# A recommender tower: steps of 256 samples, with the products of earlier steps between the lookups

## The chip, the cores and the metric

One core of one Trainium2 chip runs the whole program. The metric is the device time of one execution in microseconds (us). Engines are named as the profile names them: PE is TensorE (PEld its weight loads), DVE VectorE, ACT ScalarE, POOL GpSimd, SP SyncE.

## The reference

For each of 2048 samples it gathers 26 embedding rows of 128 numbers and has one dense vector x of 128. It forms the 27 x 27 inner products (27 vectors: x and the rows) and keeps the 351 that lie above the diagonal. The MLP follows.

```python
e = stack([tbl_f[ids[:, f]] for f in range(26)], axis=1)        # 2048 x 26 x 128
sd = einsum('bfd,bd->bf', e, x)                                   # 26 products with x
ss = einsum('bfd,bgd->bfg', e, e)[:, iu, ju]                      # 325 pairs
h = concatenate([x, sd, ss, x], axis=1)
h = maximum(h @ W_top1 + b_top1, 0)      # 607 -> 512
h = maximum(h @ W_top2 + b_top2, 0)      # 512 -> 256
y = h @ W_top3                           # 256 -> 1
```

## The kernel before

Samples go in tiles of 128, two tiles to a duo (DS = 256), four to a quad (QS = 512). Everything that a quad needs is laid down in `vecT` (feature dimension on the partitions, then sample, then the 27 vectors). Two kinds of tables fill it:

- Eight small tables (1000 rows) are held in SBUF, split in a high and a low fp32r half (`parts`), and looked up on PE: `spread_ids` (L396) repeats the ids of one feature over the partitions, DVE compares them with row numbers (`set_pack`, L253) into a one-hot pack of 1024 numbers per partition, and `lookup` (L410) multiplies. A pack is 2 chunks of 125 rows x 512 samples, so four matmuls of 512 columns; four packs are a feature, 32 packs a quad. There is a ring of six packs (`RING`): `set_pack` of use n waits for `pack_done` of use n-6. ACT copies each finished feature out (`drain_sum`, L310).
- The other 18 features are gathered by POOL with indirect DMAs (L221), 288 in all: four to a group of two features x two tiles, 9 groups a duo, a ring of six groups (`rows`). PE transposes a group with four matmuls (L426) and ACT copies it out (`drain_rows`, L316).

The order on every engine is written out by hand. Stage A of a quad runs its 32 packs on PE; after given packs come 15 of the 18 row groups (`ROWS_AFTER`) and the MLP of the quad before (`LAYER1_AFTER` and so on: layer 1 L458 and L462, layer 2 L472, layer 3 L481, transposes of the pairs L450). Stage B is the gram: per sample one product of 26 x 26 out of `vecT` (L436). A tile has two halves of 64 samples, a half fills one of the two `vec_bank` buffers, and ACT copies it to `dots` (`drain_gram`, L325). `vecT` exists once, so no lookup of the next quad is drained before the gram of this one is over, and PE issues the gram without lookups between. DVE turns a tile of `dots` (`turn`: one transpose L264, then 26 copies L270 into `pairs`) at packs 5 and 7 of the next quad.
PE's own loop, and the waits ahead of the gram:

```python
for p in range(PACKS):
    if p % PER == 1:
        spread_ids(NH * q + p // PER + 2)     # waits pack_set >= PER * (use - 1)
    lookup(q, p)
    for j in ROWS_AFTER.get(p, []):
        transpose_rows(q, j)
    if q:
        mlp(q - 1, p)
pe.wait_ge(sum_drained, NH * (q + 1))
pe.wait_ge(x_copied, q + 1)
```

In quad 0 the eight tables arrive as well (480 + 20 KB each, three raw buffers); DVE splits one (L238, L242) ahead of the four packs that need it, and ACT makes its high half (L296). After the last quad only its MLP is left.

## Time and profile before

| | us |
|---|---|
| runs shown (3) | 550.11, 551.03, 553.82; median 551.03 |
| the profiled execution, its own time | 554.1 |
| its span, first to last instruction | 552.2 |
| mean granted TensorE clock | 0.805 of full speed |

The span is what the views of the trace cover; 1.9 us of the execution's own time lie around it. Full speed of PE's clock is 2.4 GHz, a granted 0.5 is 1.2 GHz. Matmuls are pipelined: the time from one start to the next says more than the mean length of one.

### The profile page before, as it was taken

The page shows a single profiled execution, that of the slowest core. Times are in us where ns is not written, and L with a number is a line of the kernel's source. Part 1 is how long each engine was busy: PE and PEld are TensorE (multiplying, and loading weights), DVE is VectorE, ACT ScalarE, POOL GpSimd, SP SyncE. Part 2 cuts the span into 40 slices and gives each one's busy share as a digit, 9 for nine tenths or more (in the row PEclk, how much of TensorE's full clock was granted, in tenths as well). Part 3 has the DMA queues.
Part 4 walks back from the last instruction along what each step waited for, and adds up shares of the span by engine and source line. Part 5 has one row for each costly group of instructions (what it writes and reads, how often), then busy time and mean ns, then how long its engine had stood idle before and what let it go on. Part 6 is the DMA issues. An engine that isn't in the chain of part 4 may idle for free.

```text
span 552.2 us, 12229 instructions
## 1 busy us (share of the span) xinstructions
PE 375.6 (68%) x5424; PEld 294.6 (53%) x5424; DVE 231.4 (42%) x579; ACT 174.7 (32%) x221; POOL 277.3 (50%) x297
## 2 busy tenths in 40 slices
PE   2650587426379959955489859954559859975697
PEld 0430455315267648745367647743448648864576
DVE  5610687414144553532244443632226535505500
ACT  1400345313132343421142333421215324443122
POOL 7777467563416656753516756663416666610000
PEclk9985599667579979976579969965569978996699
DMA  8522263110102112211101112211101111100000
GB/s 201 142 53 52 67 198 89 40 49 23 40 8 53 44 38 53 66 35 37 40 10 52 44 38 52 63 43 30 27 20 40 43 43 49 43 18 4 4 0 1
DMA packets 11596, 26.93 MB, mean 49 GB/s; under 512 B 5033, under 2 KB 5161, under 8 KB 11409
## 3 DMA queue, kind: packets, MB, share of 16 engines
q0 software_dynamic: 9216, 18.89, 13.4%
q1 hardware_dynamic: 2328, 7.27, 4.9%
q8 instruction: 42, 0.69, 0.5%
q14 instruction: 10, 0.07, 0.0%
HBM read 26.14 MB, written 0.01 MB: 47 GB/s over the span
## 4 chain that ended last, share of the span: by engine, by line
PE 62%; issue 21%; ACT 7%; another core or an unknown queue 7%; DMA 2%; POOL 1%; DVE 1%
PE sum_bank L410 22%; PE vec_bank L436 12%; PE work_bank L462 8%; PE vec_bank L426 6%; PE work_bank L472 5%; ACT vecT L316 3%; PE work_bank L458 3%; PE work_bank L481 2%; ACT vecT L310 2%; PE work_bank L450 2%; PE id_bank L396 1%; DMA rows<-in_tbl,ids_all 1%; ACT parts L296 1%; ACT late L342 1%
## 5 line engine op out<-in xcount | busy, mean ns | idle before, releaser
L221 POOL DMA_INDIRECT rows<-in_tbl,ids_all x288 | 274.6, 953 | 207.7 <-PE vec_bank L426 86.5
L253 DVE TENSOR_TENSOR onehot<-id_bank,row_f 125x1024 fp32r<-125x1024 f32 x128 | 151.6, 1220 | 170.6 <-PE sum_bank L410 72.8
L410 PE MATMUL sum_bank<-onehot,parts 125*128 125x512 f32 x512 | 166.0, 459 | 4.2 <-DVE onehot L253 4.2
L436 PE MATMUL vec_bank<-vecT 128*26 128x26 f32 x4096 | 68.7, 215 | 81.4 <-issue 73.7
L410 PEld LDWEIGHTS sum_bank<-onehot,parts 125*128 125x128 f32 x512 | 103.1, 213 | 30.8 <-issue 12.2
L316 ACT COPY vecT<-vec_bank 128x512 f32<-128x512 f32 x72 | 85.3, 1200 | 80.7 <-remote 49.0
L436 PEld LDWEIGHTS vec_bank<-vecT 128*26 128x26 f32 x4096 | 56.4, 131 | 96.4 <-issue 85.0
L264 DVE STREAM_TRANSPOSE late<-late 128x832 f32<-128x832 f32 x16 | 28.7, 1793 | 113.6 <-ACT late L325 113.6
L426 PE MATMUL vec_bank<-ident,rows 128*128 128x128 f32 x288 | 52.1, 314 | 10.6 <-DMA rows<-in_tbl,ids_all 3.8
L325 ACT COPY late<-vec_bank 128x416 f32<-128x416 f32 x32 | 16.2, 507 | 123.1 <-PE vec_bank L436 123.1
L426 PEld LDWEIGHTS vec_bank<-ident,rows 128*128 128x128 f32 x288 | 41.2, 162 | 23.9 <-issue 11.7
L310 ACT COPY vecT<-sum_bank 128x512 f32<-128x512 f32 x32 | 39.1, 1221 | 37.8 <-PE sum_bank L410 20.7
L462 PE MATMUL work_bank<-late,w_all 117*128 117x256 f32 x192 | 48.4, 388 | 2.3 <-issue 2.2
L342 ACT ACTIVATE late<-work_bank,w_all 128x256 f32<-128x256 f32 x48 | 22.9, 477 | 66.6 <-PE work_bank L462 24.4
L462 PEld LDWEIGHTS work_bank<-late,w_all 117*128 117x128 f32 x192 | 37.0, 194 | 9.3 <-issue 3.3
L396 PE MATMUL id_bank<-idsT,pick 8*128 8x512 f16 x32 | 13.4, 426 | 41.7 <-DVE onehot L253 25.7
L270 DVE COPY late<-late 128x1 f32<-128x1 f32 (+25 forms) x416 | 35.2, 186 | 3.6 <-issue 1.9
L481 PE MATMUL work_bank<-w_all,late 128*128 128x1 f32 x64 | 12.4, 315 | 29.5 <-ACT late L342 26.9
L472 PE MATMUL work_bank<-late,w_all 128*128 128x256 f32 x128 | 30.2, 380 | 1.3 <-ACT late L342 1.3
L396 PEld LDWEIGHTS id_bank<-idsT,pick 8*128 8x128 f16 x32 | 2.9, 92 | 50.2 <-DVE onehot L253 27.2
L481 PEld LDWEIGHTS work_bank<-w_all,late 128*128 128x128 f32 x64 | 11.8, 276 | 32.1 <-ACT late L342 29.3
L472 PEld LDWEIGHTS work_bank<-late,w_all 128*128 128x128 f32 x128 | 23.6, 189 | 5.3 <-ACT late L342 2.1
(23 smaller groups left out, 99.2 us busy)
## 6 DMA issues: line engine op xcount, KB each, us to landing
rows<-in_tbl,ids_all POOLq DMA_INDIRECT x288
late<-in_tbl SPq DMA_DIRECT2D x8, 480.0 KB
w_all<-in_weights SPq DMA_DIRECT2D x1, 1540.0 KB
xT<-in_dense_t SPq DMA_DIRECT2D x4, 256.0 KB
late<-in_weights SPq DMA_DIRECT2D x1, 256.0 KB
ids_all<-in_ids SPq DMA_DIRECT2D x1, 208.0 KB, 3.0
late<-in_tbl SPq DMA_DIRECT2D x8, 20.0 KB
vecT<-in_ids_t SPq DMA_DIRECT2D x1, 64.0 KB
```

Source lines behind the costliest of these rows:

```text
L221: nc.gpsimd.indirect_dma_start(rows[:, g % ROWS_RING, n, t, :], None, tables[f], bass.IndirectOffsetOnAxis(ids_all[:, TD * d + t, f:f + 1], 0)
L253: nc.vector.tensor_tensor(onehot[:, use % RING, :, :], bass.AP(got.tensor, got.offset, [got.ap[0], [0, PW], [1, QS]]), bass.AP(numbers.ten ...
L264: nc.vector.transpose(turned.rearrange("p c i -> p (c i)"), dots[:, tile % 2, :, :].rearrange("p i c -> p c i")).then_inc(tile_turned, 1)
L270: last = nc.vector.tensor_copy(pairs[:, tile % 2, pairs_of(c, c + 1)], turned[:, c, 0:c + 1])
L310: nc.scalar.copy(vecT[:, :, place(ONEHOT[n] + 1)], sum_bank[use % 2][:]).then_inc(sum_drained, 1)
L316: nc.scalar.copy(vecT[:, s0:s0 + DS, low:high_place + 1:high_place - low].rearrange("d s v -> d v s"), vec_bank[use % 2][:].rearrange("d ( ...
L410: last = nc.tensor.matmul(sum_bank[into % 2][:], parts[:, part, CH_AT[n] + c0 + c, :], onehot[:, use % RING, c, :], start=(p % PER == 0 an ...
L426: last = nc.tensor.transpose(vec_bank[into % 2][:, (n * TD + t) * P:(n * TD + t + 1) * P], rows[:, use % ROWS_RING, n, t, :], ident[:])
L436: last = nc.tensor.matmul(vec_bank[into % 2][BL * j:BL * j + GC, i * GC:(i + 1) * GC], vecT[:, s, 0:GC], vecT[:, s, 1:VECS], start=True, s ...
L462: last = nc.tensor.matmul(out, w1p[:, b, cols], pairsT[0:KP, b, :], start=False, stop=(b == KT - 1))
L472: last = nc.tensor.matmul(work_bank[use % 2][:, 0:DS], w2_sb[:, b, m * P:(m + 1) * P], h1[:, b, :], start=(b == 0), stop=(b == M1 - 1))
L481: last = nc.tensor.matmul(work_bank[use % 2][:, t:t + 1], h2[:, b, t * P:(t + 1) * P], w3_sb[:, b:b + 1], start=(b == 0), stop=(b == M2 - 1))
```

## The change

- The unit of work is a duo (`d`, 8 of them) with 16 packs instead of a quad with 32. A pack is 4 chunks x 256 samples: eight matmuls of 256 columns in `lookup`, the same 1024 numbers for DVE. `spread_ids` and `drain_sum` move 256 columns each and run twice as often.
- `vecT` has two buffers of 256 samples in the space of the one of 512. In step `d` (10 steps: `DUOS + 2`) PE goes through sixteen slots; a slot has the pack of duo `d`, a row group in nine of the sixteen, a quarter of a half of the gram of duo `d-1` (16 samples, 32 matmuls), and in given slots pair transposes and single matmuls of the MLP of duo `d-2`. Steps 8 and 9 have no lookups.
- Row transposes have one bank (`vec_bank`), the gram one (`gram_bank`), each with its own semaphores; before, both shared two. `dots`, `pairs`, `pairsT`, `h1`, `h2` stay as they are.
- Turns: tile 1 of duo `d-2` after pack 5 and tile 0 of duo `d-1` after pack 13. Pair transposes after slots 3 and 13, layer 1 in slots 4 to 9, layer 2 in 10 to 12, layer 3 after slot 15.
- Layer 3 has `w3` as weights and streams `h2` (2 products of 256 columns into one row) instead of 4 products with one column; `y` is kept in two single-partition rows and stored by two DMAs.
- `xT` has four buffers of 256. The weights come in one DMA without waiting for the tables to be split; a second iota and cast (`row_8`) and one matmul that fills `gram_bank` are added at the start. In POOL's loop only the semaphore it waits for is another.

The diff, cut to its core (helpers that were only renamed from `q` to `d` are left out, as are semaphore declarations and assertions):

```diff
-    TD, TQ = 2, 4
-    DUOS, QUADS = TILES // TD, TILES // TQ
-    DS, QS = TD * P, TQ * P
+    TD = 2
+    DUOS = TILES // TD
+    DS = TD * P
...
-    PER = 4
-    PACKS = PER * NH
-    PW = CH_MAX // PER
-    assert all(c == CH_MAX for c in CH)
+    PACKS = 2 * NH
+    PW = CH_MAX // 2
...
-    ROWS_IN_A = 15
+    HALVES = 2 * TD
+    XS = 4
+
     ROWS_AFTER = {}
-    for j in range(ROWS_IN_A):
-        ROWS_AFTER.setdefault(max(j, 31 - 5 * (ROWS_IN_A - 1 - j) // 2), []).append(j)
-    ROWS_AFTER_GRAM = {0: [15], 1: [16, 17]}
-    TURN_AFTER = {RING - 1: [0, 1, 2], RING + 1: [3]}
-    PAIRS_AFTER_GRAM = {2: 0, 3: 1}
-    LAYER1_AFTER = {1: (0, 0), 3: (0, 1), 5: (0, 2), 7: (0, 3), 17: (1, 0), 19: (1, 1), 21: (1, 2), 23: (1, 3)}
-    LAYER2_AFTER = {9: (0, 0), 11: (0, 1), 25: (1, 0), 27: (1, 1)}
-    LAYER3_AFTER = {13: 0, 29: 1}
-    PAIRS_AFTER = {14: 2, 15: 3}
-
-    VEC_USES = 2 * GROUPS + 2 * TQ
-
-    def rows_at(q, j):
-        return VEC_USES * q + {15: 17, 16: 20, 17: 21}.get(j, j)
-
-    def gram_at(q, t, h):
-        return VEC_USES * q + {0: 15, 1: 18, 2: 22, 3: 24}[t] + h
+    for j in range(GROUPS):
+        ROWS_AFTER.setdefault((2 * j + 1) * (PACKS - 1) // (2 * GROUPS), []).append(j)
+    TURN_AFTER = {RING - 1: (2, 1), RING + 7: (1, 0)}
+    PAIRS_AFTER = {3: (2, 1), 13: (1, 0)}
+    LAYER1_AFTER = {4: [(0, 0), (0, 1), (0, 2)], 5: [(0, 3), (1, 0), (1, 1)], 6: [(1, 2), (1, 3), (2, 0)],
+                    7: [(2, 1), (2, 2), (2, 3)], 8: [(3, 0), (3, 1)], 9: [(3, 2), (3, 3)]}
+    LAYER2_AFTER = {10: [(0, 0), (0, 1), (0, 2)], 11: [(0, 3), (1, 0), (1, 1)], 12: [(1, 2), (1, 3)]}
+    LAYER3_AFTER = 15
+
+    NW = TD + M1 + M2 + 1
+
+    def pairs_at(d, t):
+        return NW * d + 1 if t else max(NW * d - 1, 0)
+
+    def layer1_at(d, m):
+        return NW * d + 2 + m
+
+    def layer2_at(d, m):
+        return NW * d + 2 + M1 + m
+
+    def layer3_at(d):
+        return NW * (d + 1) - (d == DUOS - 1)
...
-        xT = sb("xT", [P, 2, QS])
-        vecT = sb("vecT", [P, QS, VECS])
+        xT = sb("xT", [P, XS, DS])
+        vecT = sb("vecT", [P, 2, DS, VECS])
...
-        onehot = sb("onehot", [RP, RING, PW, QS], fp32r)
-        idsT = sb("idsT", [NH, BATCH], fp16)
-        ids_i = vecT[0:NH, :, :].rearrange("n s v -> n (s v)")[:, 0:BATCH].bitcast(i32)
-        y_cols = sb("y_cols", [P, TILES])
+        onehot = sb("onehot", [RP, RING, PW, DS], fp32r)
+        lines = sb("lines", [65, BATCH], fp16)
+        idsT = lines[0:NH, :]
+        y_half = [lines[32 * (h + 1):32 * (h + 1) + 1, :].bitcast(fp32) for h in range(2)]
...
-        vec_bank = [bank(f"vec_bank{n}") for n in range(2)]
+        vec_bank, gram_bank = bank("vec_bank"), bank("gram_bank")
...
-            sp.dma_start(w_all[:], weights[:, HID1:]).then_inc(weights_loaded, 16)
-            sp.wait_ge(low_set, NH)
-            sp.wait_ge(high_set, NH)
-            sp.dma_start(w1x2, weights[:, 0:HID1]).then_inc(w1x2_loaded, 16)
-            for q in range(1, QUADS):
-                load_x(q)
+            sp.wait_ge(ids_cast, 1)
+            sp.dma_start(w_all[:], weights).then_inc(weights_loaded, 16)
+            for d in range(1, DUOS):
...
+            for h in range(2):
+                sp.dma_start(y.rearrange("(p h t) o -> h p (t o)", p=P, h=2)[h:h + 1],
+                             y_half[h].rearrange("o (p t) -> o p t", p=P)).then_inc(y_stored, 16)
...
-                    freed = g - ROWS_RING
-                    pool.wait_ge(vec_filled, rows_at(freed // (2 * GROUPS), freed % (2 * GROUPS)) + 1)
+                    pool.wait_ge(tr_filled, g - ROWS_RING + 1)
...
-                if p % PER == 0:
-                    dve.wait_ge(id_filled, NH * q + n + 1)
+            def set_pack(d, p):
+                n, c0, w = p // 2, (p % 2) * (CH[p // 2] // 2), CH[p // 2] // 2
+                use = PACKS * d + p
+                if p % 2 == 0:
+                    dve.wait_ge(id_filled, NH * d + n + 1)
...
+                    if p in TURN_AFTER:
+                        lag, t = TURN_AFTER[p]
+                        if 0 <= d - lag < DUOS:
+                            turn(TD * (d - lag) + t)
...
+                    if 1 <= d <= DUOS and p % 4 == 3:
+                        drain_gram(d - 1, p // 8, p // 4 % 2)
+                    if p in PAIRS_AFTER:
+                        lag, t = PAIRS_AFTER[p]
+                        if 0 <= d - lag < DUOS:
+                            drain_pairs(d - lag, t)
+                    if d >= 2:
+                        drain_layers(d - 2, p)
...
-                    pe.wait_ge(pack_set, PER * (use - 1))
-                nc.tensor.matmul(id_bank[use % 2][:], pick[:, n, :],
-                                 idsT[:, q * QS:(q + 1) * QS], start=True, stop=True).then_inc(id_filled, 1)
-
-            def lookup(q, p):
-                n, c0 = p // PER, (p % PER) * PW
-                use, into = PACKS * q + p, NH * q + n
-                if q == 0 and p % PER == 0:
+                    pe.wait_ge(pack_set, 2 * (use - 1))
+                nc.tensor.matmul(id_bank[use % 2][:, 0:DS], pick[:, n, :],
+                                 idsT[:, d * DS:(d + 1) * DS], start=True, stop=True).then_inc(id_filled, 1)
...
-                for c in range(PW):
+                for c in range(w):
                     for part in range(PARTS):
-                        last = nc.tensor.matmul(sum_bank[into % 2][:],
+                        last = nc.tensor.matmul(sum_bank[into % 2][:, 0:DS],
                                                 parts[:, part, CH_AT[n] + c0 + c, :], onehot[:, use % RING, c, :],
-                                                start=(p % PER == 0 and c == 0 and part == 0),
-                                                stop=(p % PER == PER - 1 and c == PW - 1 and part == PARTS - 1))
+                                                start=(p % 2 == 0 and c == 0 and part == 0),
+                                                stop=(p % 2 == 1 and c == w - 1 and part == PARTS - 1))
...
+            def gram(d, p):
+                t, h, part = p // 8, p // 4 % 2, p % 4
+                if p == 0:
+                    pe.wait_ge(sum_drained, NH * (d + 1))
+                    pe.wait_ge(tr_drained, GROUPS * (d + 1))
+                    pe.wait_ge(x_copied, d + 1)
+                if part == 0 and (d or p):
+                    pe.wait_ge(gram_drained, HALVES * d + p // 4)
+                for i in range(part * HALF // 4, (part + 1) * HALF // 4):
                     for j in range(4):
-                        s = t * P + BL * j + h * HALF + i
-                        last = nc.tensor.matmul(vec_bank[into % 2][BL * j:BL * j + GC, i * GC:(i + 1) * GC],
-                                                vecT[:, s, 0:GC], vecT[:, s, 1:VECS], start=True, stop=True)
-                last.then_inc(vec_filled, 1)
+                        last = nc.tensor.matmul(gram_bank[BL * j:BL * j + GC, i * GC:(i + 1) * GC],
+                                                vecT[:, d % 2, t * P + BL * j + h * HALF + i, 0:GC],
+                                                vecT[:, d % 2, t * P + BL * j + h * HALF + i, 1:VECS],
+                                                start=True, stop=True)
+                if part == 3:
+                    last.then_inc(gram_filled, 1)
...
-            def layer3(d):
-                use = NW * d + W3
-                pe.wait_ge(work_drained, use)
-                for t in range(TD):
-                    for b in range(M2):
-                        last = nc.tensor.matmul(work_bank[use % 2][:, t:t + 1], h2[:, b, t * P:(t + 1) * P],
-                                                w3_sb[:, b:b + 1], start=(b == 0), stop=(b == M2 - 1))
-                last.then_inc(work_filled, 1)
...
+            def layer1(d, m, b):
+                use = layer1_at(d, m)
                 cols, out = slice(m * P, (m + 1) * P), work_bank[use % 2][:, 0:DS]
-                nc.tensor.matmul(out, w1x[:, cols], xT[:, d // 2 % 2, d % 2 * DS:(d % 2 + 1) * DS], start=True, stop=False)
-                if m == 0:
-                    pe.wait_ge(work_drained, NW * d + W1)
-                for b in range(KT):
-                    last = nc.tensor.matmul(out, w1p[:, b, cols], pairsT[0:KP, b, :],
-                                            start=False, stop=(b == KT - 1))
+                if b == 0:
+                    free_work(use)
+                    nc.tensor.matmul(out, w1x[:, cols], xT[:, d % XS, :], start=True, stop=False)
+                    return
+                if m == 0 and b == 1:
+                    pe.wait_ge(work_drained, pairs_at(d, 1) + 1)
+                last = nc.tensor.matmul(out, w1p[:, b - 1, cols], pairsT[0:KP, b - 1, :], start=False, stop=(b == KT))
+                if b == KT:
+                    last.then_inc(work_filled, 1)
...
+            def layer3(d):
+                use = layer3_at(d)
+                pe.wait_ge(work_drained, use)
+                for b in range(M2):
+                    last = nc.tensor.matmul(work_bank[use % 2][0:1, 0:DS], w3_sb[:, b:b + 1], h2[:, b, :],
+                                            start=(b == 0), stop=(b == M2 - 1))
...
+            nc.tensor.matmul(gram_bank[:], pick[:, 0, :], idsT[:, 0:512], start=True, stop=True)
...
-            for q in range(QUADS):
-                if q == 1:
+            for d in range(DUOS + 2):
+                if d == 2:
                     pe.wait_ge(w1x_summed, 1)
                 for p in range(PACKS):
-                    if p % PER == 1:
-                        spread_ids(NH * q + p // PER + 2)
-                    lookup(q, p)
-                    for j in ROWS_AFTER.get(p, []):
-                        transpose_rows(q, j)
-                    if q:
-                        mlp(q - 1, p)
-                pe.wait_ge(sum_drained, NH * (q + 1))
-                pe.wait_ge(x_copied, q + 1)
-                pe.wait_ge(vec_drained, rows_at(q, GROUPS - 1) + 1)
-                for t in range(TQ):
-                    if t == TD:
-                        pe.wait_ge(vec_drained, rows_at(q, 2 * GROUPS - 1) + 1)
-                    for h in range(2):
-                        gram(q, t, h)
-                    for j in ROWS_AFTER_GRAM.get(t, []):
-                        transpose_rows(q, j)
-                    if t in PAIRS_AFTER_GRAM:
-                        transpose_pairs(q, PAIRS_AFTER_GRAM[t])
-            for p in range(PACKS):
-                mlp(QUADS - 1, p)
+                    if d < DUOS:
+                        if p % 2:
+                            spread_ids(NH * d + p // 2 + 2)
+                        lookup(d, p)
+                        for j in ROWS_AFTER.get(p, []):
+                            transpose_rows(d, j)
+                    if 1 <= d <= DUOS:
+                        gram(d - 1, p)
+                    if p in PAIRS_AFTER:
+                        lag, t = PAIRS_AFTER[p]
+                        if 0 <= d - lag < DUOS:
+                            transpose_pairs(d - lag, t)
+                    if d >= 2:
+                        layers(d - 2, p)
...
```

## Rows read from the trace of the kernel before

**Rows 1.** The page's span, busy time of each engine

```profile
span 552.2 us, 12229 instructions
...
PE 375.6 (68%) x5424; PEld 294.6 (53%) x5424; DVE 231.4 (42%) x579; ACT 174.7 (32%) x221; POOL 277.3 (50%) x297
```

**Rows 2.** Windows: length, busy PE, PEld, DVE, ACT, POOL (instructions), PEclk, DMA, GB/s

```profile
0.00:110.00 110.00, 54.80 (x198) 37.35 (x198) 58.05 (x55) 33.25 (x32) 75.40 (x84) 0.80 0.40 105
110.00:158.00 48.00, 22.29 (x1034) 17.43 (x1032) 14.85 (x84) 9.56 (x13) 20.23 (x22) 0.64 0.13 33
158.00:245.00 87.00, 71.52 (x323) 56.72 (x324) 41.04 (x59) 31.86 (x41) 52.99 (x56) 0.90 0.18 46
245.00:285.00 40.00, 22.64 (x1044) 18.29 (x1043) 13.05 (x82) 9.81 (x14) 15.14 (x16) 0.63 0.12 30
...
491.00:521.00 30.00, 16.30 (x1043) 14.39 (x1044) 11.59 (x81) 9.05 (x14) 0.00 (x0) 0.72 0.02 4
521.00:552.00 31.00, 26.49 (x119) 21.25 (x118) 3.80 (x27) 7.58 (x18) 0.00 (x0) 0.94 0.00 1
```

**Rows 3.** The page's costliest groups: busy, mean ns, idle before and what ended it

```profile
L221 POOL DMA_INDIRECT rows<-in_tbl,ids_all x288 | 274.6, 953 | 207.7 <-PE vec_bank L426 86.5
...
L410 PE MATMUL sum_bank<-onehot,parts 125*128 125x512 f32 x512 | 166.0, 459 | 4.2 <-DVE onehot L253 4.2
L436 PE MATMUL vec_bank<-vecT 128*26 128x26 f32 x4096 | 68.7, 215 | 81.4 <-issue 73.7
...
L264 DVE STREAM_TRANSPOSE late<-late 128x832 f32<-128x832 f32 x16 | 28.7, 1793 | 113.6 <-ACT late L325 113.6
...
L270 DVE COPY late<-late 128x1 f32<-128x1 f32 (+25 forms) x416 | 35.2, 186 | 3.6 <-issue 1.9
```

**Rows 4.** Timeline of PE, inside one lookup stage: start, length, what, count, idle before

```profile
215.03 0.39 PE L396 MATMUL id_bank<-idsT,pick 8*128 8x512 f16 x1
215.34 1.20 PE L410 MATMUL sum_bank<-onehot,parts 125*128 125x512 f32 x4
216.38 0.60 PE L426 MATMUL vec_bank<-ident,rows 128*128 128x128 f32 x4
216.81 0.60 PE L458 MATMUL work_bank<-xT,w_all 128*128 128x256 f32 x2
...
218.36 2.19 PE L410 MATMUL sum_bank<-onehot,parts 125*128 125x512 f32 x8
```

**Rows 5.** The chain of waits, first gather and that lookup stage: start, length, what

```profile
8.96 7.19 DMA rows<-in_tbl,ids_all
...
218.72 1.84 PE sum_bank L410 x8
```

**Rows 6.** Waits of POOL: who for whom, us in total, times, longest

```profile
POOL rows L221 <- issue: 80.0, 257, 1.6
```

**Rows 7.** Timeline of PE, the second gram block (245 to 285 us)

```profile
247.38 0.26 PE L436 MATMUL vec_bank<-vecT 128*26 128x26 f32 x6 [0.47 <-issue]
```

**Rows 8.** Timeline of PE, the last gram block, POOL without work

```profile
499.59 1.29 PE L436 MATMUL vec_bank<-vecT 128*26 128x26 f32 x128 [1.79 <-issue]
...
513.08 0.99 PE L450 MATMUL work_bank<-ident,late 128*117 128x128 f32 x3
514.00 1.41 PE L436 MATMUL vec_bank<-vecT 128*26 128x26 f32 x99
```

**Rows 9.** The page's DMA queues: the queue that brings instructions

```profile
q8 instruction: 42, 0.69, 0.5%
```

**Rows 10.** Timeline of PE around a third-layer product

```profile
199.36 1.86 PE L481 MATMUL work_bank<-w_all,late 128*128 128x1 f32 x8 [6.44 <-ACT late L342]
```

**Rows 11.** Timeline of DVE in the first stage

```profile
59.48 1.22 DVE L253 TENSOR_TENSOR onehot<-id_bank,row_f 125x1024 fp32r<-125x1024 f32 x1 [19.08 <-remote]
```

**Rows 12.** Timeline of PE in the first stage

```profile
32.60 2.43 PE L410 MATMUL sum_bank<-onehot,parts 125*128 125x512 f32 x8
60.76 0.60 PE L396 MATMUL id_bank<-idsT,pick 8*128 8x512 f16 x1 [25.74 <-DVE onehot L253]
```

272 lines of the change are left out of this document (121 added, 151 removed).

## The prediction

> **What bounds the kernel now.** I read the page's totals first [rows 1]: PE is busy 375.6 of 552.2 us, POOL 277.3, DVE 231.4, ACT 174.7. No engine is full, so the bound changes with the stage, and the windows say how [rows 2]. The reader is to see two kinds of stretch. In a lookup stage (158 to 245) PE is busy 71.5 of 87 us at a granted 0.90. In a gram block (245 to 285) it is busy 22.6 of 40 us at 0.63, while DVE, ACT and POOL work 13.1, 9.8 and 15.1 us. The first gram block takes 48 us, the last 30.
>
> What fills a gram block is in the groups and the timelines. The 4096 gram matmuls are busy 68.7 us, and PE is idle another 81.4 us before them, 73.7 of these "issue": no semaphore and no engine explains them [rows 3]. Within a block a burst is followed by a trickle, six matmuls within 0.26 us after 0.47 us of idle time [rows 7]. In the last block, where POOL has nothing to do, it is cleaner: 128 matmuls with their 128 weight loads in 1.29 us, and 1.79 us of idle time ahead [rows 8]. That is 256 instructions per stop. The instruction queue moved 0.69 MB in 42 packets [rows 9], 16 KB each, for 10,848 matmuls and weight loads [rows 1]: 258 per packet. I read the stops as PE waiting for its next block of instructions. A gram is 2048 instructions and runs with some 90 others, 8.4 blocks: 30/8.4 = 3.6 us a block in the last one, 40/8.4 = 4.8 in the second, where POOL's share is 15.1/40 = 0.38. The Trainium skill (Runtime: NRT & Kernel Launch, § Instruction fetch mechanics) has the same blocks of 256 instructions and calls the cost of passing from one to the next mostly hidden; by that rule a gram block would last as long as its bursts, about 13 us, and the trace's 30 to 48 speak against it.
>
> In the lookup stage the missing time sits mostly before layer 3: PE idles 6.44 us until ACT has drained layer 2 [rows 10], about once in each duo's MLP.
>
> **The change part by part.** First PE's work in a full step (lookups of duo d, gram of d-1, MLP of d-2), from starts one after the other.
> - Lookup: two packs, eight matmuls of 512 columns, are 1.84 us of the chain [rows 5], 0.23 each. The step has 128 matmuls of 256 columns. Half of 0.23 is 0.115; I take 0.12: 15.4 us. From below: a row group, 4 x 128 columns with 4 weight loads, takes 0.43 us to the next product [rows 4], so a weight load and its stream together 0.108, and 256 columns of one pass the same: 13.8 us. From above, an exposed weight load adds up to 0.107 to each (rival 1).
> - Ids: 0.31 from an id product to the lookup behind it [rows 4], of which the stream is 0.21; with halved columns 0.2, and about 0.1 ahead of it: 8 x 0.3 = 2.4 us.
> - Row groups: 9 x 0.43 = 3.9 us, unchanged.
> - Gram: 512 matmuls. The burst gives 10 ns each [rows 8], the whole group's busy time 17 [rows 3]; I take 12.5: 6.4 us. From below 5.1; from above the present 40 us for 1024 make 20.
> - Going from full products to gram and back: from 513.08 to 514.00 there are three pair transposes (0.21 each at the lower clock) and 0.28 for both turns [rows 8]. Sixteen slots: 4.5 us, which is new. Bounds: nothing and twice that.
> - MLP: eight matmuls of layer 1 stand between 216.81 and 218.36 [rows 4]; with the lookup's late start, 0.217 each. 48 of layers 1 and 2 are 10.4 us, layer 3 is 4 x 0.217 = 0.9 instead of 8 one-column ones in 1.86 [rows 10], pairs 0.7: 12.0 us.
>
> The sum is 44.6 us a step with no stall, at the upper clock level.
>
> The other engines, per step. POOL: 36 gathers of 953 ns [rows 3] with 80.0/257 = 0.31 us between them [rows 6] make 45.4 us. That is as long as PE's sum, so POOL is the second floor. DVE: 231.4/8 = 29 us, unchanged in size; a turn is 1.8 for the transpose and 35.2/16 = 2.2 for the copies [rows 3], 4.0 us. ACT: 174.7/8 = 22 us, plus under 1 for the fixed part of twice as many `drain_sum`. Both have cover of 15 us and more in a step, and I cost their edits at nothing.
>
> Instruction blocks: a step holds 742 matmuls and their loads, 1484 instructions, 5.8 blocks; spread over the slots, one lasts 7.7 us. Supply is 3.6 us without gathers and 4.8 with POOL busy 0.38. POOL will be busy 0.76 of the time (0.95 of 1.26); the line through the two points gives 3.6 + 0.76 x 3.2 = 6.0 us. That is under 7.7, so the stops should vanish, but not by much. A slot's 32 gram matmuls are also a quarter of the 128 that ran before a stop.
>
> What remains of stalls. Gone: most of the "issue" time, and the layer 3 wait, as layer 3 follows layer 2 by three slots (8 us) instead of two packs. New: the single `vec_bank` (ACT needs 1.2 us for a group, and a slot or more lies between two); the single `gram_bank`, drained while the next pack runs. Behind a wait of PE on either stand the rest of the slot and the next pack, and DVE, ACT and POOL wait for these. Then the pairs of tile 1 in slot 3: DVE turns only after pack 5, which needs the ids that PE issues in slot 1: 2.8 + 0.3 + 0.7 + 2.4 + 4.0 = 10.2 us from the step's start, against slot 3's end at 10.5. Up to 1 us can be lost there. In the lookup stage before, what is idle beside two layer 3 waits of about 6 is 87 - 71.5 - 12 = 3.5 us. I take 5 us a step for all of it: 49.5 us. The bounds of a step are 45.4 (POOL) and 55.
>
> Clock: the lookup stage is granted 0.90 while PE is busy 82% of it, the gram block 0.63 while it is busy 56% [rows 2]. With PE at 90% in every step I expect the upper level nearly throughout, and price nothing.
>
> The stages then:
> - Step 0. Before, the first stage took 110 us [rows 2] with a hole in it: PE, done with its packs at 35, waits 25.7 us for DVE until 60.76 [rows 12], and DVE stood until 59.48 [rows 11], for `pack_done` of packs that PE shows finished. PE waited in `spread_ids`, which asked for packs two ahead; the new one asks for none ahead, but DVE's wait stays. Without a hole, the gathers set the end: 4 + 9 x 5.04 + 3 for the landing = 52 (the first group takes 7.2 to land, beside the tables [rows 5]). With one of 26 us or so, 75 to 85. I take 75.
> - Step 1 (no MLP): 44.6 - 12.0 + 5 = 38.
> - Steps 2 to 7: 6 x 49.5 = 297.
> - Step 8 (gram and MLP, no lookups): 6.4 + 4.5 + 12.0 and four waits of 1 for `gram_bank`: 27.
> - Step 9: drain 0.6, turn 4.0, pairs and drain 1, MLP with its hand-overs 12: 18. Before, the MLP of two duos took 31 [rows 2].
> - Two y stores in many short rows instead of one: between 0 and 5, I take 2.5.
>
> 75 + 38 + 297 + 27 + 18 + 2.5 = 457.5 of span, 459.4 with the 1.9 around it, against the profiled 554.1. The median of the runs shown is 3.1 below that; I keep the ratio: 457 us.
>
> **The rivals.**
> 1. Weight loads show. At 256 columns stream and load are equally long, 0.107. If the loads don't overlap, 1024 lookups at 0.214 instead of 0.12 cost 96 us more: 553 us, no gain. Against it: a row group's 0.108 per product holds load and stream in the time of one [rows 4]. The Trainium skill (TensorE: Matmul & The Clock Gate, § The mechanism) says that a load overlaps running matmuls only when its row group differs, which would give this rival; the row speaks against it.
> 2. Slower: the supply of instructions falls behind. PE's matmuls and loads grow from 10,848 to 11,874, 46 blocks. It decides from 7.7 us a block on; at 11 us a step is 64 us, and 75 + 45 + 6 x 64 + 50 = 554. The first gram block has 48/8.4 = 5.7 us a block with POOL at 20.2/48 = 0.42 [rows 2]; the line through this and the second passes 11 us at a share of 0.66: 555 to 600 us. Against it: the first block still has other transfers and a clock of 0.64, and the longer line gives 6.0.
> 3. The hole does not come and PE keeps up with POOL: the last gather lands at 4 + 288 x 1.26 + 3 = 370; 370 + 3 + 27 + 18 + 2.5 + 1.9: 422 to 438 us.
> 4. Late hand-overs stay, 6 us in each step as before layer 3 now: 480 to 505 us.
> 5. The change does not do what it says: the stops stay between slots, at half their present 40 us for 1024: 10 us a step, 515 us.
>
> **How the numbers follow.** Forecast (440 to 479) 0.48; rival 3 0.14; rival 4 0.17; rival 5 0.06; rival 1 0.04; rival 2 0.11. The range 425 to 520 leaves out rivals 1 and 2 and the low end of 3. A measurement of this kernel tells about 1% from no change. Faster by over 1%: 0.84; within: 0.05; slower: 0.11.
>
> **What would show it.** The gram's "issue" idle falls from 73.7 us to under 15. Lookup matmuls start every 0.12 us. The granted clock is over 0.9. A step lasts 47 to 52 us. About 46 instruction packets. Layer 3 waits under 2 us each. The prediction is wrong if lookup starts are 0.2 apart, if PE stands idle with "issue" in each slot, or if the hole of the first stage grows.

## The result, and the profile after

The changed kernel takes 655.6 us (median of 4 runs, 649.2 to 656.3), the kernel before 552.4 beside it: ratio 1.184, interval 1.174 to 1.194. It is slower by 18%, where 457 was forecast.

The page of the changed kernel: totals, clock, instruction queue and chain.

```profile
span 654.5 us, 13364 instructions
...
PE 480.1 (73%) x5937; PEld 383.3 (59%) x5937; DVE 229.6 (35%) x580; ACT 188.1 (29%) x257; POOL 279.0 (43%) x298
...
PEclk9886567566678887887889878878788787689899
...
q8 instruction: 47, 0.77, 0.5%
...
PE 65%; issue 18%; another core or an unknown queue 7%; ACT 4%; POOL 3%; DMA 1%; DVE 1%; DVEq 0%
...
L223 POOL DMA_INDIRECT rows<-in_tbl,ids_all x288 | 276.2, 959 | 296.8 <-PE vec_bank L419 205.6
L256 DVE TENSOR_TENSOR onehot<-id_bank,row 125x1024 fp32r<-125x1024 f32 x128 | 150.8, 1220 | 373.1 <-remote 200.4
L406 PE MATMUL sum_bank<-onehot,parts 125*128 125x256 f32 x1024 | 209.1, 362 | 14.1 <-issue 9.9
...
L433 PE MATMUL gram_bank<-vecT 128*26 128x26 f32 x4096 | 94.6, 200 | 91.1 <-issue 85.4
```

DVE and POOL do the work that they did [rows 1], ACT has 13 us more (188.1 for 174.7), and the gathers cost the same 0.96 us each [rows 3]. PE is busy 104 us longer for 513 more matmuls, at a clock of 0.79 instead of 0.805. The gram's "issue" idle (time for which the profile shows no reason) was to vanish and has grown from 73.7 to 85.4 us. The new waits are on the other side: DVE stands 200 us before its one-hots for "remote" (a signal whose sender the profile did not find), and POOL 206 us for row groups that PE consumes late.

The windows give two stretches, one of the middle and the end, where no gather is left.

```profile
200.00:266.00 66.00, 50.98 (x615) 40.89 (x615) 24.34 (x68) 19.23 (x26) 29.24 (x32) 0.80 0.13 34
...
580.00:655.00 75.00, 62.95 (x1092) 48.72 (x1090) 22.39 (x114) 23.81 (x41) 0.00 (x0) 0.93 0.01 2
```

With gathers the granted clock is 0.80 and PE is busy 77% of the time; at the end it is 0.93 and 84%. The stages, from the PE timeline: the first gram matmul starts at 85.9 us, the last slot of step 7 ends at 606.8, step 8 lasts 24.1 us and the rest 23.6. So steps 1 to 7 take 521 us, 74.4 each, where 335 in all was forecast.

Within a step, PE's timeline and POOL's over the same microseconds:

```profile
239.94 1.27 PE L406 MATMUL sum_bank<-onehot,parts 125*128 125x256 f32 x8
241.14 0.60 PE L433 MATMUL gram_bank<-vecT 128*26 128x26 f32 x23
242.24 0.24 PE L433 MATMUL gram_bank<-vecT 128*26 128x26 f32 x4 [0.49 <-issue]
243.63 0.33 PE L433 MATMUL gram_bank<-vecT 128*26 128x26 f32 x5 [1.16 <-issue]
245.06 1.88 PE L406 MATMUL sum_bank<-onehot,parts 125*128 125x256 f32 x8 [1.10 <-issue]
```

```profile
239.44 0.94 POOL L223 DMA_INDIRECT rows<-in_tbl,ids_all  x1 [4.28 <-PE vec_bank L419]
240.68 0.94 POOL L223 DMA_INDIRECT rows<-in_tbl,ids_all  x1 [0.30 <-issue]
241.93 0.94 POOL L223 DMA_INDIRECT rows<-in_tbl,ids_all  x1 [0.30 <-issue]
243.18 0.94 POOL L223 DMA_INDIRECT rows<-in_tbl,ids_all  x1 [0.30 <-issue]
```

This is the trickle of [rows 7] again, four or five matmuls after each gap, now within a slot of 32. It begins in the middle of POOL's four gathers and ends a microsecond after them; when POOL waits again (244.1 to 248.1), PE runs freely. The next group of gathers (248.1 to 252.8) has its trickle at 251.5 to 253.7, the one after (257.3 to 262.0) at 261.5 to 263.

The first stage shows the same for signals. PE, DVE and POOL:

```profile
40.07 1.20 PE L406 MATMUL sum_bank<-onehot,parts 125*128 125x256 f32 x8
51.73 1.09 PE L419 MATMUL vec_bank<-ident,rows 128*128 128x128 f32 x4 [10.46 <-ACT vecT L315]
...
53.07 3.35 PE L406 MATMUL sum_bank<-onehot,parts 125*128 125x256 f32 x16
73.43 1.09 PE L419 MATMUL vec_bank<-ident,rows 128*128 128x128 f32 x4 [17.02 <-ACT vecT L315]
```

```profile
43.58 1.23 DVE L245 TENSOR_TENSOR parts<-late 125x1024 fp32r<-125x1024 f32 x1
72.82 2.36 DVE L256 TENSOR_TENSOR onehot<-id_bank,row 125x1024 fp32r<-125x1024 f32 x2 [28.02 <-remote]
```

```profile
67.14 0.94 POOL L223 DMA_INDIRECT rows<-in_tbl,ids_all  x1 [0.30 <-issue]
72.35 0.94 POOL L223 DMA_INDIRECT rows<-in_tbl,ids_all  x1 [4.27 <-remote]
```

PE's id products had ended at 53.1 and its packs at 56.4. DVE, idle since 44.8 (PE's own row transposes and id products came late, too), moves only at 72.82, 20 us after the id product that it waited for, when POOL has stood since 68.1. The same can be read in the kernel before: DVE went on at 59.48 and PE at 60.76 [rows 11, 12], 4 to 5 us after the last gather of POOL's first unbroken run (issued at 54.37) had ended.

The semaphore events in the trace say the same more sharply. For each PE product that raises a semaphore I take the time from its end, as the profile models it, to the next event of that semaphore. In the result 153 of the 319 such products up to the last gather have an event over 1 us late, the longest 19.7 us; of the 49 behind the last gather none. The stops go with the gathers as well. Of the groups of four gathers 28 stand alone, POOL idle for over 3 us before and 2.5 us after. Each of them has two to four stops of PE of over 0.3 us, 84 in all, that end 1 to 6 us after its first gather was issued, and none in the microsecond before it, in which 840 gram matmuls start. The kernel before shows it from block to block: 33, 25 and 26 stops in the three gram blocks with gathers, 8 in the last one without.

So the hole that I had priced and left unexplained, and the trickle, have one thing in common: gathers under way. That is the theory for the experiments; the rivals to it are the supply of instructions to a longer program, and transfers as such.

### The profile page after: what moved, and what is told of

It is laid out like the page before. It is cut to its first block, busy times and chain, and to the rows that moved or that the text cites. A ratio compares the mean times of both kernels' runs of the same rounds, so it can differ in the third digit from the quotient of the medians.

```text
span 654.5 us, 13364 instructions
## 1 busy us (share of the span) xinstructions
PE 480.1 (73%) x5937; PEld 383.3 (59%) x5937; DVE 229.6 (35%) x580; ACT 188.1 (29%) x257; POOL 279.0 (43%) x298
## 3 DMA queue, kind: packets, MB, share of 16 engines
q0 software_dynamic: 9216, 18.89, 11.4%
q1 hardware_dynamic: 2904, 7.27, 4.0%
## 4 chain that ended last, share of the span: by engine, by line
PE 65%; issue 18%; another core or an unknown queue 7%; ACT 4%; POOL 3%; DMA 1%; DVE 1%; DVEq 0%
PE sum_bank L406 24%; PE gram_bank L433 12%; PE work_bank L462 7%; PE vec_bank L419 6%; PE work_bank L472 6%; PE work_bank L458 3%; POOL rows L223 3%; PE id_bank L392 2%; ACT vecT L315 2%; PE work_bank L449 2%; PE work_bank L481 1%; ACT vecT L309 1%; DMA rows<-in_tbl,ids_all 1%; DVE late L272 1%
## 5 line engine op out<-in xcount | busy, mean ns | idle before, releaser
L256 DVE TENSOR_TENSOR onehot<-id_bank,row 125x1024 fp32r<-125x1024 f32 x128 | 150.8, 1220 | 373.1 <-remote 200.4
L406 PE MATMUL sum_bank<-onehot,parts 125*128 125x256 f32 x1024 | 209.1, 362 | 14.1 <-issue 9.9
L406 PEld LDWEIGHTS sum_bank<-onehot,parts 125*128 125x128 f32 x1024 | 180.6, 255 | 32.5 <-issue 26.0
L433 PE MATMUL gram_bank<-vecT 128*26 128x26 f32 x4096 | 94.6, 200 | 91.1 <-issue 85.4
L433 PEld LDWEIGHTS gram_bank<-vecT 128*26 128x26 f32 x4096 | 66.0, 113 | 130.7 <-issue 117.3
L315 ACT COPY vecT<-vec_bank 128x512 f32<-128x512 f32 x72 | 85.9, 1193 | 111.3 <-PE vec_bank L419 75.5
L309 ACT COPY vecT<-sum_bank 128x256 f32<-128x256 f32 x64 | 42.9, 670 | 211.7 <-remote 135.7
L458 PE MATMUL work_bank<-xT,w_all 128*128 128x256 f32 x64 | 26.1, 496 | 1.2 <-issue 1.2
L392 PE MATMUL id_bank<-lines,pick 8*128 8x256 f16 x64 | 21.5, 338 | 5.9 <-DVE lines L276 5.9
L324 ACT COPY late<-gram_bank 128x416 f32<-128x416 f32 x32 | 17.0, 530 | 26.7 <-PE gram_bank L433 13.6
L449 PE MATMUL work_bank<-ident,late 128*117 128x128 f32 x48 | 14.0, 406 | 9.1 <-DVE late L272 6.3
```

The costliest lines, as they stand in the source:

```text
L256: nc.vector.tensor_tensor(onehot[:, use % RING, 0:w, :], bass.AP(got.tensor, got.offset, [got.ap[0], [0, w], [1, DS]]), bass.AP(numbers.te ...
L309: nc.scalar.copy(vecT[:, d % 2, :, place(ONEHOT[n] + 1)], sum_bank[use % 2][:, 0:DS]).then_inc(sum_drained, 1)
L315: nc.scalar.copy(vecT[:, d % 2, :, low:high_place + 1:high_place - low].rearrange("d s v -> d v s"), vec_bank[:].rearrange("d (v s) -> d v ...
L392: nc.tensor.matmul(id_bank[use % 2][:, 0:DS], pick[:, n, :], idsT[:, d * DS:(d + 1) * DS], start=True, stop=True).then_inc(id_filled, 1)
L406: last = nc.tensor.matmul(sum_bank[into % 2][:, 0:DS], parts[:, part, CH_AT[n] + c0 + c, :], onehot[:, use % RING, c, :], start=(p % 2 == ...
L433: last = nc.tensor.matmul(gram_bank[BL * j:BL * j + GC, i * GC:(i + 1) * GC], vecT[:, d % 2, t * P + BL * j + h * HALF + i, 0:GC], vecT[:, ...
```

## The experiments

Every kernel ran beside the kernel before on the same chip, and that showed something first: there are chips where the kernel before takes 433 to 435 us (four of them here) and chips where it takes 552 to 558 (two, and that of the result). I call them the first and the second kind; the kind did not change within a chip's runs.

### Is it the gathers, and is it their bytes?

**a_nogather, b_nogather**: only the first groups are gathered, in the changed kernel and in the one before.

```
-            for g in range(DUOS * GROUPS):
+            for g in range(ROWS_RING):
...
-                pe.wait_ge(gathered[use % ROWS_RING], 16 * FG * TD * (use // ROWS_RING + 1))
+                pe.wait_ge(gathered[use % ROWS_RING], 16 * FG * TD)
```

> The changed kernel, with only the first six gather groups issued (24 of 288 gathers); later steps transpose the same rows again, so most of the gathered features are left out of the result. Theory G (gathers in flight slow PE's stream and make its signals late): the issue idle time before gram matmuls falls from 85.4 us to under 15, the granted clock rises over 0.9, a step takes about 45 to 48 us, the whole 400 to 440 us. Rival I (the longer program: 11,874 matmuls and weight loads can't be supplied faster): nothing changes, 630 to 660 us. Rival C (the small-column matmuls and the half clock cost it by themselves): 600 to 650 us.

> The kernel before, with only the first six gather groups issued; later stages transpose the same rows again. Theory G: the gram blocks of 48, 40 and 44 us become like the last one, 30 us, the layer 3 waits of about 6 us and the hole of 26 us in the first stage go: 440 to 480 us. Rival I: 545 to 555 us.

**a_plain, b_plain**: the same bytes into the same tiles, each group behind the same wait for its place in the ring, as SP's plain DMAs. Two things differ beside the issuing engine: a DMA reads 128 neighbouring rows of a table instead of those that the ids name, and the transfers go in other pieces (44,376 packets of the hardware queue, against 9,216 of the software queue and 2,904 of the hardware one with the gathers).

```
+                        k = (TD * (g // GROUPS) + t) % 7 * P
+                        sp.dma_start(rows[:, g % ROWS_RING, n, t, :], tables[f][k:k + P, :]
+                                     ).then_inc(gathered[g % ROWS_RING], 16)
...
-                        nc.gpsimd.indirect_dma_start(
-                            rows[:, g % ROWS_RING, n, t, :], None, tables[f],
-                            bass.IndirectOffsetOnAxis(ids_all[:, TD * d + t, f:f + 1], 0)
-                        ).then_inc(gathered[g % ROWS_RING], 16)
```

> The changed kernel with each gather replaced by a plain DMA of 128 table rows of 512 B each, issued by SP: the same bytes and the same pieces, the rows not those that the ids name. If the DMA traffic itself slows PE (theory G1), 630 to 660 us with the trickle as before. If it is POOL's gather instructions and their descriptors (G2), as without gathers, 400 to 450 us.

> The kernel before with each gather replaced by a plain DMA of 128 table rows issued by SP. G1 (traffic): about 550 us. G2 (POOL's gathers): 440 to 490 us.

All four on one chip of the first kind, before at 434.3: a_nogather 388.1 (ratio 0.894, 0.888 to 0.900), b_nogather 419.4 (0.964, 0.958 to 0.971), a_plain 385.2 (0.886, 0.881 to 0.892), b_plain 424.0 (0.977, 0.971 to 0.983). Without gathers the changed kernel is 31 to 39 us faster than the one before without gathers. This could not yet be set against the 655.6, since the chip was another.

**after_again, before_again**: both kernels unchanged, on one chip.

> The changed kernel, unaltered. In the runs before this one the kernel before took 434 us beside the experiments and 552 beside the first measurement of the change, so the price of the gathers is not the same everywhere. Theory G (gathers in flight take time from PE; how much depends on the chip or on the time): where the kernel before takes about 434 us, the change is faster, 385 to 410 us; where it takes 552, about 655. Rival N (the gathers' price is that of the changed program alone): slower by 15 to 20% wherever it runs.

> The kernel before, unaltered, for a profile of it beside the others. G: as its own runs here, 1.00; if they take about 434 us, the first stage has no hole of 26 us, there is no trickle within the gram blocks, and layer 3 waits 1 to 2 us.

Before 433.7 (0.997), the changed kernel 423.7 (0.976, 0.971 to 0.980): **on this chip, of the first kind, the change is faster by 2.4%.** The page of after_again:

```profile
span 421.2 us, 13364 instructions
...
PEclk9977698989999999999999999999999999998989
...
POOL 57%; issue 18%; PE 18%; DMA 3%; DVE 2%; ACT 1%; DVEq 0%
...
L223 POOL DMA_INDIRECT rows<-in_tbl,ids_all x288 | 276.7, 961 | 88.3 <-issue 86.9
...
L433 PE MATMUL gram_bank<-vecT 128*26 128x26 f32 x4096 | 53.1, 190 | 0.2 <-ACT late L324 0.2
```

and of before_again:

```profile
span 432.7 us, 12229 instructions
...
L436 PE MATMUL vec_bank<-vecT 128*26 128x26 f32 x4096 | 59.6, 207 | 45.7 <-issue 35.0
```

Here the stops do vanish, 35.0 us of "issue" to none, and POOL's back-to-back gathers carry the chain. A few slots of after_again, from PE's timeline:

```profile
206.10 0.70 PE L458 MATMUL work_bank<-xT,w_all 128*128 128x256 f32 x2
206.64 1.03 PE L462 MATMUL work_bank<-late,w_all 117*128 117x256 f32 x4
207.60 0.28 PE L392 MATMUL id_bank<-lines,pick 8*128 8x256 f16 x1
207.81 1.22 PE L406 MATMUL sum_bank<-onehot,parts 125*128 125x256 f32 x8
210.11 0.66 PE L419 MATMUL vec_bank<-ident,rows 128*128 128x128 f32 x4 [1.08 <-DMA rows<-in_tbl,ids_all]
```

PE waits for the gathered rows: 34.6 us in 21 such waits. Of POOL's 88.3 idle us 86.9 are its own issue time, so it hardly ever waits for PE.

**a_half, a_plain_2**: of the groups after the sixth every second is left out (156 gathers stay), and the plain version once more.

```
+                if g >= ROWS_RING and g % 2:
+                    continue
```

> The changed kernel with every second gather group after the sixth left out (its slot's rows are transposed again), 156 gathers instead of 288. If POOL is the floor of the changed kernel where the kernel before takes 434 us, it goes down to the 385 to 392 us of the kernel without gathers. Where the kernel before takes about 550 us: theory G (time lost in proportion to gathers in flight) gives half of the excess of 656 over 388, 510 to 540 us; rival I (program length) 630 to 660.

> The changed kernel with plain DMAs from SP for the gathers, once more, for the case that the kernel before takes about 550 us beside it. G1 (traffic of the rows slows PE there): 600 us or more. G2 (POOL's gather instructions with their descriptors do): 385 to 400 us as on the other chip. Where the kernel before takes 434 us: 384 us again.

On another chip of the first kind, before at 434.2: a_half 395.7 (0.912, 0.905 to 0.919), a_plain_2 385.0 (0.887, 0.881 to 0.893). Leaving out 132 of the 288 gathers takes back 28 of the 39 us, where an equal price for each gather would give 18. Together with POOL's chain above I read that as POOL's length, not something that each gather does to PE; the two times come from two chips of the first kind.

**a_plain_3**: on a chip of the second kind, the test that matters.

> The changed kernel with plain DMAs from SP for the gathers, for a chip on which the kernel before takes about 550 us. G1 (movement of the rows): 600 us or more there. G2 (POOL's gather instructions and descriptors): 385 to 400. Beside a kernel before of 434 us: 385, nothing new.

384.7 beside a kernel before of 558.3 (0.688, 0.684 to 0.691). Its page:

```profile
span 383.0 us, 13364 instructions
...
PE 80%; DVE 13%; ACT 2%; issue 1%; DMA 1%; SPq 0%; DVEq 0%
...
L438 PE MATMUL gram_bank<-vecT 128*26 128x26 f32 x4096 | 52.6, 189 | 0.2 <-ACT late L329 0.2
```

The same program for PE, DVE and ACT, the same bytes, no gather instructions: 385 us on both kinds of chip. So the second kind's 270 us are the price of gathering by POOL; the longer program, its weight loads and the amount of data moved cost nothing there by themselves. Whether it is the software path or the scattered addresses of the rows no run divides.

Gathers could still act on PE by slowing the supply of its instructions, and a_plain_3, which has none, can't tell. The packets of the instruction queue speak against it. In the result they take 1.1 us each (median; 1.5 at most), as in a_plain_3 (1.1, 1.6) and after_again (1.1, 1.7). PE stops 134 times before gram products for 47 packets, and of the 136 stops of over 0.3 us just 23 begin within 2 us after a packet does, about as many as an even spread gives; in before_again it is 29 of 34.

The late signals are gone with the gathers, too. With plain transfers on the second kind (a_plain_3) each of the 368 semaphore events stands within 0.1 us of the end of its product. In after_again, with all gathers on the first kind, 7 are over 1 us late, where the trace lacks five events of the semaphore that 6 of these belong to.

The Trainium skill (DMA: Bandwidth & Descriptors, § SWDGE vs HWDGE vs iDMA) has GpSimd compute its descriptors in software and write them to rings in SBUF, a path that DMAs issued from SP don't touch. The pages of the profile agree as to the queues (software_dynamic with the gathers, hardware_dynamic alone without), and that is where the runs divide the kernels; no run shows the rings. How a gather comes to delay PE's products and signals, and why only some chips show it, no run here tells.

**after_again_2, a_nogather_2**: controls.

> The changed kernel, unaltered, on another chip. Beside a kernel before of 434 us: 0.97 to 0.98, 421 to 426 us. Beside one of 550 us: 1.17 to 1.20.

> The changed kernel without gathers after the sixth group, once more, in case the kernel before takes about 550 us beside it. G: 385 to 400 us there as well, so that all of the 268 us above it are the gathers'. Rival I (program length, small matmuls): 600 us or more. Where the kernel before takes 434 us: 388 us again.

The changed kernel on another chip of the second kind: 656.6 beside 553.8 (1.186, 1.180 to 1.191), the first result again. a_nogather_2 ran on a chip of the first kind: 388.9 beside 433.2 (0.900, 0.894 to 0.907), and says only that 388 holds there.

### What is spreading the gram worth?

**a_block, a_block_2**: the changed kernel with its gram in one piece at the start of each step, all else in slots.

```
-    TURN_AFTER = {RING - 1: (2, 1), RING + 7: (1, 0)}
+    TURN_AFTER = {3: (2, 1), RING + 7: (1, 0)}
...
+                if 1 <= d <= DUOS:
+                    for p in range(PACKS):
+                        gram(d - 1, p)
```

> The changed kernel with the gram of the step behind not in quarters between the packs but all at once at the start of the step (and the turn of tile 1 after pack 3 instead of pack 5). If the spreading is what gains (instruction blocks of 3.6 us, stops between bursts), each step has 3 to 4 stops of 2 us and three waits for the one gram bank of 1 us: 8 to 11 us a step, 65 to 90 us over the changed kernel. If the spreading only adds turns between full and small products (4.5 us a step in the prediction), it is at most 30 us over it, or under it.

> The changed kernel with the gram in one piece, with all gathers. Where the kernel before takes about 550 us: if the spread gram is what suffers from gathers in flight (trickle in each slot), it comes back to 550 to 600; if every PE product near a gather suffers, as many gathers are in flight as before, 640 to 680. Beside a kernel before of 434: 442 again.

**a_block_nogather**: that with the edit of a_nogather.

> The changed kernel with its gram in one piece at the start of each step, and no gathers after the first six groups. Against the 388 us of the changed kernel without gathers: if spreading the gram over the slots saves the stops between instruction blocks and the waits for the one gram bank, 388 + 8 to 9 steps of 4 to 6 us, 420 to 440 us. If POOL's floor alone was what the gram in one piece ran into (442 against 424), 390 to 400. Where the kernel before takes 550 us, theory G gives the same numbers, rival I 600 or more.

First kind: a_block 441.7 beside 435.0 (1.016, 1.010 to 1.023), so spreading is worth 441.7 - 423.7 = 18 us there. The other two ran on chips of the second kind. a_block_nogather: 425.6 beside 553.8 (0.768, 0.764 to 0.772), 37 us above the 388 of a_nogather; those were taken on the first kind, but by a_plain and a_plain_3 the kinds agree when nothing is gathered. Its trace shows the second kind's mark in small: it has 24 gathers up to 38 us, 9 of PE's semaphore events until then are over 1 us late, and of the 347 behind them none. a_block_2: 594.5 beside 558.3 (1.062, 1.059 to 1.066): with gathers on the second kind the gram in one piece is *faster* than spread, by 62 us against the 656.6 of the other such chip (ratios 1.062 and 1.186 to the kernel before). Their pages, a_block_2 first, a_block_nogather second:

```profile
span 597.0 us, 13364 instructions
...
PE 53%; another core or an unknown queue 19%; issue 12%; ACT 10%; POOL 4%; DMA 1%; ACTq 0%
...
L434 PE MATMUL gram_bank<-vecT 128*26 128x26 f32 x4096 | 61.5, 215 | 85.8 <-issue 45.4
```

```profile
L434 PE MATMUL gram_bank<-vecT 128*26 128x26 f32 x4096 | 53.1, 207 | 46.5 <-issue 29.2
```

The stops of the gram in one piece are there without gathers, too, as in b_nogather:

```profile
L436 PE MATMUL vec_bank<-vecT 128*26 128x26 f32 x4096 | 49.0, 205 | 56.6 <-issue 47.7
```

So two things wear the name "issue": stops after some 256 instructions of dense small matmuls, on every chip, gathers or not, which spreading removes; and stops while gathers are under way, on the second kind alone, which it does not. The gram blocks of the kernel before show them apart: 8, 7, 8 and 8 stops in before_again, where 23 or 24 gathers stand in each of the first three blocks and none in the last, and 33, 25, 26 and 8 on the second kind.

**b_hold**: the kernel before, with four ring refills held until the gram block is over, so that POOL should stand in it.

```
-                    pool.wait_ge(vec_filled, rows_at(freed // (2 * GROUPS), freed % (2 * GROUPS)) + 1)
+                    q0, j0 = freed // (2 * GROUPS), freed % (2 * GROUPS)
+                    use = gram_at(q0, TQ - 1, 1) if j0 >= ROWS_IN_A - 1 else rows_at(q0, j0)
+                    pool.wait_ge(vec_filled, use + 1)
```

> The kernel before with POOL held during the gram blocks: the four gather groups that would refill the ring then wait for the end of the block. Where the kernel before takes about 434 us, POOL loses time it needs (45 us a duo of its 50): 440 to 470 us, slower. Where it takes about 550 us, theory G: three gram blocks go from 40 to 48 us towards 30, against gathers that come later, 530 to 555 us.

It ran on the first kind: 439.7 beside 433.2 (1.017, 1.009 to 1.025), gram "issue" 38.7 us against 35.0 in before_again. POOL was hardly quiet, though: behind as it is on this kind, it still issues 17 or 18 gathers in each of the first three blocks, for 23 or 24, and stands only in the last 6 to 8 us. So b_hold shows what late gathers cost, 6 us. That a quiet POOL does not shorten the stops here is shown by the last gram block of before_again (no gathers, 8 stops and 13 us of them) and by b_nogather.

### Do 256 columns show the weight loads?

**b_cols256, b_cols256_2**: the kernel before with each lookup matmul cut in two.

```
+                        for s0 in (0, DS):
+                            last = nc.tensor.matmul(sum_bank[into % 2][:, s0:s0 + DS],
+                                                    parts[:, part, CH_AT[n] + c0 + c, :], onehot[:, use % RING, c, s0:s0 + DS],
```

> The kernel before with each lookup matmul of 512 columns cut in two of 256: 512 more matmuls and weight loads, the same columns. If weight loads hide (0.12 each, prediction): 512 x 2 x 0.12 - 512 x 0.23 = 5 us more, 1.01. If they show: 512 x 0.107 = 55 us more, 1.10 to 1.13.

> The kernel before with each lookup matmul cut in two of 256 columns, for a chip on which the kernel before takes about 555 us. If the number of lookup instructions is what makes a kernel lose more to gathers there, 580 to 610 us (1.05 to 1.10). If it is the place of the gram alone, 1.00 to 1.02. Beside a kernel before of 434 us: 1.006 again.

437.3 beside 435.0 (1.006, 1.003 to 1.010) and 435.1 beside 433.0 (1.001, 0.997 to 1.005), both on the first kind. The lookups of b_cols256 and of before_again:

```profile
L411 PE MATMUL sum_bank<-onehot,parts 125*128 125x256 f32 x1024 | 160.5, 306 | 3.7 <-DVE onehot L253 3.7
```

```profile
L410 PE MATMUL sum_bank<-onehot,parts 125*128 125x512 f32 x512 | 157.4, 440 | 3.4 <-DVE onehot L253 3.4
```

512 more matmuls and loads keep PE busy 3 us longer. Rival 1 wanted 0.094 us for each of 1024, 96 us.

**b_plain_2**, b_plain once more, again on the first kind.

> The kernel before with plain DMAs from SP for the gathers, for such a chip. G2: 420 to 430 us, so that the gathers cost it 130 us there, against 270 in the changed kernel. If the kernel before has another slowness of its own there: over 450.

422.9 beside 433.0 (0.980, 0.972 to 0.987), as b_plain.

## Why the prediction was wrong

The step that failed is "Instruction blocks": I put the "issue" time down to PE waiting for its next block of instructions, drew a line through two gram blocks against POOL's share, got "6.0 us" a block at a share of 0.76, "under 7.7, so the stops should vanish". Two causes lay under one name. The one I read, 256 instructions per stop [rows 8], is real, and the change removes it (35.0 us of "issue" to 0 on the first kind; 37 us of time between a_block_nogather and a_nogather). The other, the trickle of [rows 7], follows the gathers on the second kind, where the rows that I had were taken. Of POOL's influence I made a slower supply; what the runs show are stops and late signals beside the gathers themselves, whatever the length of the program. The line is refuted from both ends: after_again has POOL at a share of 0.74 (232 of 313 us) in steps 1 to 7 and no stops, the result has 0.42 (217 of 521) and 85 us of them; and on the first kind a gram block of the kernel before lasts as long with 23 gathers in it (29.4, 29.2, 29.3 us) as without (29.5). Two of the prediction's own signs of being wrong came: "issue" stops through the slots, and a longer hole in the first stage, 28.0 us of DVE for 19.1 [rows 11].

- **PE's sum of 44.6 us a step without stalls**: right, if a little high. Without gathers a full step takes 43.6 us with its stalls (a_nogather, starts of gram 1 and 2 at 80.7 and 124.3), and step 1, forecast at 32.6 without them, 30.3. An uncovered gram slot is 0.35 us for 32 matmuls, 11 ns each against my 12.5.
- **POOL's floor of 45.4**: right; after_again has 312.5 us for seven steps, 44.6 each, and POOL leads its chain. On the first kind rival 3 came true, to its number (422 to 438; 423.7): no hole, PE keeping up.
- **Weight loads**: hidden, 0.12 was right. At the upper clock eight lookups take 1.22 us to their last end in either trace. In the result many start 0.21 apart, but so they do at half the clock.
- **Five us of stalls a step**: wrong by a factor of six. Steps 1 to 7 were 32.6 + 6 x 44.6 = 300 us without stalls and took 521, 31.5 us more each. Against a_nogather, whose PE does the same work in 289 us, busy 281 of them at a clock of 1.00, the result has PE busy 406 us at 0.79: 124 us more busy and 107 us more idle. The idle part is mostly "issue" (all of PE's "issue" waits of the result together are 110 us); how much of the busy part is the clock and how much products drawn out by the trickle the runs don't divide.
- **Step 0 at 75**: 85.9. I took the hole as a fixed 26 us and let it stand; in both traces it lasts as long as POOL issues without a pause. Calling a hole "unexplained" should have widened the range upward: the same unexplained thing could come back in every step.
- **Steps 8 and 9 at 27 and 20.5**: 24.1 and 23.6, on either kind of chip, 47.7 in sum for 47.5. Where no gather is left, each term is right within 3 us; that the two misses cancel is luck.
- **Clock**: over 0.9 forecast, 0.79 found; 0.96 in after_again. It is lower in the stretches where PE stands more (0.80 at a busy share of 77%, 0.93 at 84%), so I read it as a consequence, one that adds to the loss; that wasn't tested by itself.
- **Layer 3 waits under 2 us**: right, 1.5 us in 2 waits over the whole of the result.
- **Rival 2**, slower, at 0.11: right in sign and in that gathers are in it. That PE's longer program alone overtakes the supply is refuted by a_plain_3: the same 47 packets of instructions, 385 us on such a chip. That the gathers slow the supply is contradicted by the packets, as quick in the result as elsewhere, and by 134 stops for 47 packets; no run tests it by itself.

The sum misses 197 us of span, 186 of them in steps 1 to 7 and 11 in step 0. ACT's edits, costed at nothing, added 13 us of busy time; where POOL leads the chain (after_again) ACT has 1% of it.

**What stays open.** On the second kind the kernel before loses about 130 us to its gathers (552 to 558 against the 419 to 424 of b_nogather and b_plain, both measured on the first kind), the gram in one piece about 169 (594.5 against 425.6), the changed kernel 270. I can argue why: in blocks of packs PE has 512-column matmuls ahead of it and drains two packs ahead, so a late signal costs less, while sixteen like slots expose each hand-over and each group of gathers meets some gram matmuls. But a_block_2 keeps the changed kernel's 256-column packs and loses 100 us less, and it has more late signals (101 of 368 over 3 us, against 46 in the result), so neither the columns nor the number of late signals explains the order. No run shows what does. None of b_nogather, b_plain, b_hold and b_cols256 ran on a chip of the second kind, so whether the kernel before would take 420 there, and what its quiet POOL would give back, wasn't measured. What differs between the chips wasn't found, nor how gathers reach PE: the software path and the scattered addresses weren't varied one by one.

**The quickest version**: with its rows from plain transfers the changed order takes 385 us on the three chips where it ran, but no plain transfer does what the ids ask for. Of the kernels that compute the reference, the changed one wins by 2.4% on the first kind, the one before by 18% on the second.

## What to carry to other kernels

Before a stop of an engine is put down to one cause, lay the timelines of all engines over it in two stages that differ in one neighbour: the last gram block (no gathers, 128 matmuls a stop) and the second (gathers, 6 a stop) were two phenomena, and a line through them was no model. A change that trades long matmuls ahead for many short hand-overs has to be priced with the hand-over times that the trace shows in its worst stretch, not in its cleanest. And a forecast from one chip's trace says little about another chip when the trace holds idle time that nothing explains.

## What was unexpected of the hardware

- The kernel before took 433 to 435 us on four chips and 552 to 558 on others, and the changed one 424 and 656 to 657; with plain transfers in place of GpSimd's gathers the changed one took 385 on both kinds.
- On the second kind, gram matmuls came in fours and fives with 0.5 to 1.2 us between while POOL issued gathers, and signals of PE reached DVE 20 us (the result) and 24 us (the kernel before) after the products that raise them had ended. On such chips, behind the last gather, none of the 49 signals of the result and none of the 347 of a_block_nogather was over 1 us late.
- 288 gathers of 128 rows have a pitch of 1.25 us (0.95 and 0.30 between) on every chip; moving the same bytes by SP's DMAs costs nothing that shows in the changed kernel (a_plain 385.2, a_nogather 388.1).
- Two 256-column matmuls with two full weight loads in place of one of 512 with one cost 0.1 to 0.6% of the kernel.
